# Fillers in the second half of a recurrence with small attention pieces, and scan step widths made without GpSimd

## The reference, cut to what matters

```
dts = jnp.einsum('bkrl,kdr->bkdl', dts, dt_projs_w)
dts = jax.nn.softplus(dts + dt_projs_b[None, :, :, None])
...
dA = jnp.exp(dt[..., None] * A)
h = h * dA + (dt * u)[..., None] * Bl[:, :, None, :]
y = jnp.einsum('bkdn,bkn->bkd', h, Cl)
```

```
def step(yt, wx_t):
    yt = jax.nn.sigmoid(wx_t + yt @ Vt)
    return (yt, yt)
...
_, ys = jax.lax.scan(step, y0, jnp.swapaxes(Wx, 0, 1))
...
sim = jnp.einsum('bnhid,bnhjd->bnhij', qh * SCALE, kh) + pos
attn = jax.nn.softmax(sim, axis=-1)
out = jnp.einsum('bnhij,bnhjd->bnhid', attn, vh)
```

## Time and profile before

| | |
|---|---|
| median of three runs | 1069.36 us |
| the profiled execution | 1069.32 us |
| its span, first to last instruction | 1067.5 us |
| mean granted TensorE clock | 0.796 |
| step-width block | 36.6 to 85.4 us |
| scan block | 85.7 to about 297 us |
| recurrence, steps 0 to 516 | 453.3 to 697.4 us |
| recurrence, steps 517 to 1023 | 697.4 to 979.5 us |
| rest of the attention | from 979.8 us |

### The profile page before, as it was taken

How to read it: one execution, slowest core, us unless ns; L and a number is a source line. 1 busy time by engine, 2 the same in 40 slices (tenths; PEclk the granted TensorE clock), 3 DMA queues, 4 the chain that set the end, 5 groups by cost and what they waited for, 6 DMA issues and landing times. The chain is left out here.

```text
span 1067.5 us, 12725 instructions
## 1 busy us (share of the span) xinstructions
PE 832.8 (78%) x4855; PEld 443.8 (42%) x4897; DVE 435.2 (41%) x733; ACT 447.4 (42%) x1480; POOL 255.4 (24%) x153
## 2 busy tenths in 40 slices
PE   7907888888885877899999999978785555765886
PEld 4302333333343443344444444447453333544544
DVE  4697999999955654600000000030440000211453
ACT  4446767676725533233333333322223333224342
POOL 3377989898910000110000000000000000000310
PEclk9957999999997588899999999965555555555696
DMA  3020000000000001200000000000000000000000
GB/s 69 2 59 0 1 0 1 0 1 0 1 1 5 1 2 30 75 1 1 1 1 2 1 1 1 1 1 1 1 1 1 1 1 1 1 1 1 1 23 10
DMA packets 10022, 8.00 MB, mean 7 GB/s; under 512 B 7378, under 2 KB 8514, under 8 KB 9672
## 3 DMA queue, kind: packets, MB, share of 16 engines
q1 hardware_dynamic: 9960, 7.18, 2.8%
HBM read 5.34 MB, written 0.26 MB: 5 GB/s over the span
## 5 line engine op out<-in xcount | busy, mean ns | idle before, releaser
L850 PE MATMUL L2p_z<-L2yx,L2v 64*32 64x2 f32 x2048 | 246.8, 188 | 104.4 <-ACT L2yx L864 103.2
L864 ACT ACTIVATE L2yx<-L2p_z 32x2 f32<-32x2 f32 x1024 | 165.0, 161 | 361.3 <-PE L2p_z L850 361.3
L850 PEld LDWEIGHTS L2p_z<-L2yx,L2v 64*32 64x32 f32 x2048 | 158.8, 120 | 272.4 <-ACT L2yx L864 260.7
L852 PE MATMUL L2p_z<-stream 128*128 128x512 bf16 x491 | 190.6, 390 | 0.0
L630 POOL TENSOR_TENSOR hc<-hs,cb 128x1024 f32<-128x1024 f32 x64 | 149.5, 2357 | 20.7 <-DVE hs L613 20.5
L1507 DVE COPY xn<-L2yx 32x512 f32<-32x512 f32 (+1 forms) x2 | 0.8, 384 | 345.4 <-ACT L2yx L864 345.4
L557 PE MATMUL p_y<-hc,ident 128*128 128x512 f32 x256 | 122.8, 602 | 5.0 <-DVE y_seq L596 2.8
L1507 POOL COPY xn<-L2yx 32x128 f32<-32x128 f32 x1 | 0.3, 283 | 522.2 <-SPq L1835 522.2
L613 DVE TENSOR_TENSOR_SCAN hs<-d_a,p_bb 128x1024 f32<-128x1024 f32 x48 | 109.8, 2287 | 7.3 <-ACT d_a L580 1.1
L557 PEld LDWEIGHTS p_y<-hc,ident 128*128 128x128 f32 x256 | 47.7, 191 | 49.9 <-issue 31.4
L584 ACT ACTIVATE cb<-p_cb 128x1024 f32<-128x1024 f32 x64 | 65.0, 1016 | 6.8 <-PE p_cb L547 6.5
(11 more groups left out here) (489 smaller groups left out, 960.9 us busy)
## 6 DMA issues: line engine op xcount, KB each, us to landing
y_seq<-in_pick SPq DMA_DIRECT2D x1, 768.0 KB
b_parts<-part SPq DMA_DIRECT2D x3, 256.0 KB, 3.7
c_parts<-part SPq DMA_DIRECT2D x3, 256.0 KB, 4.4
pos<-in_pos SPq DMA_DIRECT2D x1, 512.0 KB, 3.7
ao<-in_at_o SPq DMA_DIRECT2D x1, 512.0 KB, 4.0
L1w<-in_L_w SPq DMA_DIRECT2D x1, 297.0 KB
L3w<-in_L_w SPq DMA_DIRECT2D x1, 297.0 KB
x_tok<-in_x SPq DMA_DIRECT2D x2, 128.0 KB, 3.0
```

Of the source, the lines that this page charges most:

```text
L850: pe.matmul(p_step[:, t % 2], v[:, 0:C], yx[:, NB * t:NB * (t + 1)], start=True, stop=True).then_inc(s("preact"), 1)
L852: pe.matmul(p_z[:, 1, 0:FILL], stream[:, 0:128], stream[:, 0:FILL], start=True, stop=True)
L864: act.activation(yx[0:C, NB * (t + 1):NB * (t + 2)], p_step[:, t % 2], ACT.Sigmoid).then_inc(s("state"), 1)
```

## The change

**Step widths.** GpSimd has no work in this block any more. ScalarE writes |z| and max(z, 0) straight from PSUM and takes exp(-|z|) chunk by chunk; B and C of both directions share 128 partitions, so that four chunks of the bf16 parts replace eight. VectorE makes the correction, adds it to the positive part (`above`) while ScalarE still works, and finishes with one operation for each 1024 columns (line 486). Two of the four wide products `drive = step * seq` stay at the end of the block; the two of direction 1 are GpSimd's, at units 2 and 18 of the scan. The memset of `d_a` covers one element in 128. ScalarE loads the exponential table at the start of the block and again at its end. PSUM has four buffers of each kind, SyncE issues 12 transfers in place of 6, and 16 streaming matmuls on TensorE start at the first logarithm, where 20 started after the last chunk.

**Recurrence.** Every step from 517 on has either a filler or one piece, by a small planner. Each piece is announced with a length in ns and a number of columns; `goes` adds up columns and lengths backwards and lets the piece go if enough columns lie within `WINDOW`, otherwise the step gets a filler. Pieces are cut differently: scores go in halves of 128 keys, transposes in pairs, projections in strips of 128 columns, values for two uses in one matmul.

```
-                    p_bc = ps("p_bc", [R, 2, BANK], stack=s3)
-                    p_d = ps("p_d", [128, 2, BANK], stack=s3)
+                    p_bc = ps("p_bc", [128, 4, BANK], stack=s3)
+                    p_d = ps("p_d", [128, 4, BANK], stack=s3)
...
-                            pe.wait_ge(sig["softplus"], NCH)
-                            keep_streaming(pe, p_d[:, 0], 20)
+                            pe.wait_ge(sig["log1"], 1)
+                            keep_streaming(pe, p_d[:, 0], 16)
...
+                            act.activation(ln_one[:, 1:2], ln_one[:, 1:2], ACT.Exp)
                             for i in range(NCH):
                                 k, c = cols(i)
                                 act.wait_ge(sig["step_made"], i + 1)
-                                act.activation(zd[:, k, c], p_d[:, i % 2], ACT.Identity, bias=b_dt[:, k:k + 1]).then_inc(sig["step_read"], 1)
-                                act.wait_ge(sig["bc_made"], i + 1)
-                                act.activation(part[0][:, k, c], p_bc[:, i % 2], ACT.Copy).then_inc(sig["part_hi"], 1)
-                            for i in range(NCH):
-                                k, c = cols(i)
-                                act.wait_ge(sig["neg_abs"], i + 2)
-                                act.activation(ex[:, k, c], ex[:, k, c], ACT.Exp).then_inc(sig["exp_neg"], 1)
+                                act.activation(ex[:, k, c], p_d[:, i % 4], ACT.Abs, bias=b_dt[:, k:k + 1]).then_inc(sig["abs"], 1)
+                                act.activation(above[:, k, c], p_d[:, i % 4], ACT.Relu, bias=b_dt[:, k:k + 1]).then_inc(sig["step_read"], 1)
+                                act.wait_ge(sig["abs"], i + 1)
+                                act.activation(ex[:, k, c], ex[:, k, c], ACT.Exp, scale=-1.0).then_inc(sig["exp_neg"], 1)
+                                if i < 4:
+                                    act.wait_ge(sig["bc_made"], i + 1)
+                                    act.activation(part[0][:, c], p_bc[:, i], ACT.Copy).then_inc(sig["part_hi"], 1)
...
+                            dve.wait_ge(sig["with_max"], NCH)
+                            for m in range(4):
+                                k, c = wide(m)
+                                dve.wait_ge(sig["log1"], 2 * m + 2)
+                                dve.scalar_tensor_tensor(step[:, k, c], step[:, k, c], ln_one[:, 0:1], above[:, k, c],
+                                                         ALU.subtract, ALU.add).then_inc(sig["softplus"], 1)
+                                if m in (1, 2):
+                                    product(m - 1)
...
-                        pool.memset(d_a[:], 0.0).then_inc(sig["first_decay_zero"], 1)
+                        pool.memset(d_a[:].rearrange("p u (w l) -> p (u w) l", l=L)[:, :, 0:1], 0.0).then_inc(sig["first_decay_zero"], 1)
                         for u in range(NU):
+                            if u in (2, 2 + NS):
+                                c = slice(u // NS * UC, (u // NS + 1) * UC)
+                                pool.tensor_tensor(drive[:, 1, c], step[:, 1, c], seqf[:, 1, c], ALU.mult)
...
+                            def goes(ns, columns):
+                                room, work = WINDOW - ns, columns + 8
+                                for length, did in reversed(beats):
+                                    part = min(length, room)
+                                    work += did * part / length
+                                    room -= part
+                                    if room <= 0:
+                                        break
+                                return work >= LEAST
...
-                                if t > HALF + 4:
-                                    next(others, None)
+                                if t > HALF + 4 and columns and goes(ns, columns):
+                                    beats.append((ns, columns + 8))
+                                    ns, columns = next(others, (0, 0))
+                                    continue
+                                if t > HALF + 4 and not columns:
+                                    ns, columns = next(others, (0, 0))
+                                beats.append((STEP, FILL + 8))
+                                if t < T - 1:
+                                    fill(FILL)
...
             def turn_scores(self, pe, u):
-                pe.wait_ge(sig["at_shifted"], u + 1)
                 for n in range(2):
                     s = 2 * u + n
                     for j in range(NJ):
+                        if j % 2 == 0:
+                            yield 540, 4 * 128
```

347 lines of the change are left out of this document (184 added, 163 removed).

## The result

The changed kernel takes 1009.5 us, median of four runs (1005.89 to 1013.02), beside 1069.3 us before (1065.43 to 1069.94). The ratio is 0.945, with an interval of 0.941 to 0.949. The forecast was 1012 us. The profile is of the slowest of the four, 1013.02 us.

A forecast was written before the change was run, and what follows sets the result against it. Bound: a one-matmul, one-sigmoid chain at half clock in the recurrence's second half, then the step-width block. 35.5 + 16.7 + 1.2 - 0.5 + 4.5 = 57.4 us off 1069.3 gives 1012 us; range 1003 to 1020, to 1027 with rivals' milder parts.

The forecast's parts named there:

- Term 1: Recurrence from step 517: at full clock with fillers and pieces it takes 246.5 us instead of 282.0, saving 35.5 us.
- Term 2: Step-width block: without GpSimd and with recut chains, its last wide operation ends at 68.7 us, not 85.4, saving 16.7 us.
- Term 3: Scan: an earlier start saves 1.2 us; two added GpSimd products cost 0.5 us, between 0 and 4.7.
- Term 4: Block behind the recurrence: starting at full instead of half clock saves 4.5 us, between 1 and 6.5.
- the prediction's own sign: Block behind the recurrence: the prediction is wrong if it takes as long as before despite full clock at its start.
- Rival A: Recurrence's second half: clock drops around pieces, some 10 falls that heal, costing 21 to 32 us; about 1038 us; 15%.
- Rival C: Recurrence's second half: fillers run at half clock throughout and lengthen the chain by 72 us; 1124 us; 2%.
- Rival B: Step-width block: VectorE's rounds are slower than summed, costing 9 us more; 1021 us; 11%.

The follow-up runs named there:

- the kernel with the first warmer start: Changed kernel plus 8 streaming matmuls on TensorE while x is loaded and 4 behind its transposes: 1012.46 us, ratio 0.948.
- two neighbouring kernels: Changed kernel with the planner's spacing rule off: 1146.76 us; kernel before with uncut pieces plus fillers in second-half steps without a piece: 1149.05 us.

## Why the prediction was right

**Term 1, the recurrence (35.5 us forecast, 38.0 measured).** The mechanism is as forecast; the run without fillers and the one with the spacing off show that it needs both. The step that was off is the price of the pieces, 5.0 us instead of 7.6. Projections were right (0.096 us above a plain step, 0.10 forecast). The transposes were taken from one at half clock, 0.09; at full clock a pair adds 0.046, 1.6 us less in all, and at half clock a pair adds 0.30, by the kernel without fillers. Half units of scores add 0.11, not 0.15. Neither is half of the price at half clock. An estimate that fits all of these prices: a piece adds its own time on TensorE less what the step leaves unused. At half clock one transpose adds 0.09 us and a pair 0.30, so a transpose takes 0.21 and 0.12 is unused. With half of 0.21 at full clock, the 0.046 of a pair gives 0.17 unused there. By the same sums a projection (0.41 at half clock) adds 0.10 and half a unit (0.42) 0.10 at full clock; 0.096 and 0.11 were measured. What must be halved is the piece's own time, not what it adds.

**Term 2, the step-width block (16.7 and 18.2).** Right about the TENSOR_SCALARs. How the 18.2 us divide is an estimate from the rows of before: the group of eight took 10.2 us where eight of 0.42 take 3.4, which is 6.8 us; for the last 4.8 us (80.59 to 85.39) VectorE had ended its products and the block waited for GpSimd's; the other 6.6 us are the recut chains. No run separates these. ScalarE ended its logarithms 22.5 us behind the first matmul (24.2 summed), VectorE its narrow operations 23.3 us behind it (24.6 summed); the six wide ones took 7.2 us, as summed (7.4). The sums counted too little overlap between neighbours on ScalarE: its last chunks start an operation every 0.57 us, where 0.62 was summed.

**Term 3, the scan (1.2 and -0.5).** Its start came 0.6 us closer to the block's end (2.7 us, from 3.3), half of what was forecast: the wait of 1.11 us for ScalarE's first decay is gone, but VectorE's first product waits 1.36 us for TensorE behind the block's end, 0.96 us before. The products cost nothing, by the run without them, where 0.5 us was charged. The errors cancel.

**Term 4, the last block (4.5).** The profiled pair says 4.2, but seven profiles of either kind say 86.7 - 84.1 = 2.6 us, with single blocks up to 3.7 us from their mean. What was off is the assumption that a block which starts at full clock runs at full clock: the clock falls 2.1 us into the block in the changed kernel too, and of the 11.5 us of TensorE work full clock could not take half. By the prediction's own sign, a block as long as before in spite of a full clock at its start, the kernel with the first warmer start (87.7 us) speaks against the term as a rule, and the 4.2 us of the profiled pair are in part luck. The same stretch behind the last sigmoid reads:

```profile
934.40:945.90 11.50, 9.62 (x111) 6.90 (x109) 6.87 (x32) 4.54 (x9) 6.87 (x10) 0.70 0.01 1
```

**The rivals.** Rival A was priced with a mechanism that no run of the recurrence showed. It read two earlier stretches at half clock as falls that heal by themselves; they healed in stages with other work. In the recurrence a fall lasted to its end, through 200 steps without a piece, unless a row of fillers was put in. Rival C is what a fall leads to: 0.261 us a filled step, not 0.22, and two neighbouring kernels landed there, at 1147 and 1149 us, behind a single fall in the first 4 us. It decides from 57.4 / 0.261 = 220 steps, so one fall anywhere in the first half of the stretch would have made the change a loss. That chance was put at 2%, on the strength of the first half, which has no pieces, and the condition that mattered, how many pieces stand in a row and how little array work they hold, was weighed under rival A as a matter of 21 to 32 us. The forecast was right because the spacing held, and its range of 1003 to 1027 left out the only bad case that is near; as the prediction had no row on how thin a row of pieces may be, that is in part luck. The rule of the Trainium skill cited there, a clock that swings between its levels (TensorE: Matmul & The Clock Gate, A second HAM failure mode), met neither: the clock stayed full for 505 us, or stayed half for 369 and 393 us. Nor does the trace of the first half speak against that rule, as the prediction says, for it shows hardly any of the idle time that the rule is about: TensorE is busy for 243.91 of 244.00 us in the changed kernel, and the 236.65 of 244.30 us in the earlier trace rows come with 29 records fewer. Rival B fell: the TENSOR_SCALAR takes 420 ns without GpSimd.

**The sum.** The terms give 61.8 us saved against 57.4 forecast; the profiled execution lost 5.5 us of it at its start, where the clock rose late. The bounds of the terms, added up as they stand, give 1006 to 1034 us, not the 1003 to 1022 us that the prediction states; the measured time lies in both. The changed kernel's four runs spread by some 0.4% to either side. Over the fourteen profiles the start varies by 6.6 us, the stretch ahead of the recurrence by 2.7 (155.8 to 158.5 us) and the last block by 6.4 us, partly from changes of the code; which of them makes the spread within one kernel is not shown, as each was profiled once.

## What to carry to other kernels

Where fillers hold the clock of a latency-bound chain, their worth is decided by the weakest few steps in a row, not by the average: look for the longest row of thin pieces without a filler, because one fall there can cost more than the fillers bring in the whole stretch. The same fillers did not get the clock back; a row of sixteen with nothing in between did. Before moving work from GpSimd to VectorE, compare the durations of VectorE's one-input operations beside GpSimd's work and away from it; a group at two or three times its neighbours is a gain that waits there. Look at single durations, too, as a mean can mix blocked and free ones. Take the price of a piece from a step at the clock at which it will run.

## What the runs showed of the hardware

- A diet of one small fp32 matmul and one filler a step keeps TensorE at 2.4 GHz (the 244 us of the first half, and with spaced pieces all of the recurrence, within 505 us at full clock) and, once at 1.2 GHz, keeps it there (192 such steps in 141 us, within 369 us at half clock), although TensorE's rows are busy for 135.85 of 141.0 us. 16 streaming matmuls in a row brought it back within 5.3 us.
- GpSimd's eight subtractions on 128 x 512 fp32 made VectorE's CAST 2.4 times as long (415 to 1010 ns) and its TENSOR_SCALAR more than three times (0.41 to 1.50 us) where it started behind a running subtraction, in two of eight. The blocked time stands in the profile as VectorE's own duration, which ends 0.28 us behind GpSimd's.
- The first rise of the clock in an execution varied from 11.4 to 14.5 us in ten profiles and was at 24.9 us in one, in kernels whose TensorE instructions are the same up to there; the step-width block starts up to 5.6 us later for it.
